# Rotary products from PSUM ahead of the root normalisation, in a fused attention and feed-forward kernel on Trainium2

## What is computed

```
xn = layernorm(x)
q  = (xn @ Wq.T) as 16 sub-heads of 8 numbers;  k likewise
rmsnorm(q) = q * rsqrt(mean(q*q over 8) + eps)
rotary: (x1, x2) -> (x1*c + x2*s, -x1*s + x2*c)       c, s by token
q, k = rotary(rmsnorm(q)), rotary(rmsnorm(k))
scores = q k^T, causal softmax, difference of two heads, times v, layernorm, Wproj
```

## Time and profile before

| | |
|---|---|
| median of 3 runs | 759.69 us |
| the profiled execution: span, first to last instruction | 687.9 us |
| mean granted TensorE clock | 0.950 |
| busy, PE / DVE / ACT / POOL | 590.2 / 530.8 / 496.5 / 326.7 us |
| projection stage | 0 to 116.6 us |
| attention with first feed-forward | 116.6 to 455.6 us |
| second block | 455.6 to 687.9 us |

### The profile page before, as it was taken

How to read it: one execution, slowest core, us unless ns; L and a number is a source line. 1 busy time by engine, 2 the same in 40 slices (tenths; PEclk the granted TensorE clock), 3 DMA queues, 4 the chain that set the end, 5 groups by cost and what they waited for, 6 DMA issues and landing times. The chain is left out here.

```text
span 687.9 us, 15892 instructions
## 1 busy us (share of the span) xinstructions
PE 590.2 (86%) x4825; PEld 355.3 (52%) x4826; DVE 530.8 (77%) x1425; ACT 496.5 (72%) x843; POOL 326.7 (47%) x466
## 2 busy tenths in 40 slices
PE   3576765899999999999999999977999799999960
PEld 2465554233333333333333333375877589999960
DVE  3999998687978889797888877779798856555575
ACT  2367795798989989898998999923455467777741
POOL 0224345344534344452434544252477777776661
PEclk9799998799999999999999999998899979999995
DMA  8000001000544566644466650041122233333475
GB/s 218 16 16 31 20 13 61 1 1 2 102 91 74 82 116 116 115 88 91 63 106 116 116 106 12 1 157 59 59 82 74 80 82 102 95 103 91 131 208 166
DMA packets 76265, 56.06 MB, mean 81 GB/s; under 512 B 6528, under 2 KB 70848, under 8 KB 75968
## 3 DMA queue, kind: packets, MB, share of 16 engines
q1 hardware_dynamic: 70688, 46.01, 30.8%
q0 software_dynamic: 4352, 8.99, 3.9%
q10 hardware_dynamic: 1184, 0.56, 0.3%
HBM read 15.36 MB, written 28.65 MB: 64 GB/s over the span
## 5 line engine op out<-in xcount | busy, mean ns | idle before, releaser
L787 ACT ACTIVATE attend_prob<-attend_ring 128x1024 f32<-128x1024 f32 (+1 forms) x320 | 280.0, 951 | 16.4 <-PE attend_ring L933 14.4
L731 POOL TENSOR_SCALAR_AFFINE_SELECT attend_prob<-attend_prob 128x256 f32<-128x256 f32 x256 | 118.0, 485 | 141.4 <-ACT attend_prob L787 140.8
L953 PE MATMUL attend_ps_o<-attend_prob,attend_v_slot 128*32 128x512 f32 (+3 forms) x1536 | 156.6, 496 | 0.0
L933 PE MATMUL attend_ring<-attend_qk_slot 32*128 32x512 f16 (+3 forms) x672 | 80.1, 329 | 8.1 <-ACT attend_prob L787 6.3
L1907 POOL DMA_INDIRECT expert_outputs<-routed_linear_gated,routed_expert_goal_now x72 | 70.3, 977 | 29.7 <-issue 23.9
L1033 POOL DMA_INDIRECT slots<-rows,slot_index x64 | 62.1, 971 | 37.3 <-issue 33.2
L933 PEld LDWEIGHTS attend_ring<-attend_qk_slot 32*128 32x128 f16 x672 | 22.4, 91 | 106.7 <-ACT attend_prob L787 37.6
L1935 DVE TENSOR_TENSOR outed_linear_head_normed<-outed_linear_head_normed,routed_linear_ps_c 128x256 f32<-128x256 f32 x72 | 30.2, 420 | 41.3 <-ACT outed_linear_head_normed L2029 36.8
L953 PEld LDWEIGHTS attend_ps_o<-attend_prob,attend_v_slot 128*32 128x32 f32 x1536 | 33.7, 108 | 44.9 <-issue 37.7
L2076 PE MATMUL routed_linear_ps_c<-outed_linear_head_normed,head_turned 128*128 128x128 f32 x384 | 52.5, 281 | 1.1 <-ACT head_turned L2010 1.1
L369 POOL TENSOR_TENSOR project_parts_q<-project_rotated_q,project_parts_q 128x1024 f16<-128x1024 f32 x8 | 17.6, 2201 | 68.9 <-ACT project_parts_q L417 68.9
(11 more groups left out here) (291 smaller groups left out, 1281.8 us busy)
## 6 DMA issues: line engine op xcount, KB each, us to landing
slots<-attend_zeros SPq DMA_DIRECT2D x24, 715.0 KB, 10.2
attend_qk_slot<-qk_parts SPq DMA_DIRECT2D x14, 512.0 KB, 3.1
x_pairs<-slots SPq DMA_DIRECT2D x72, 65.0 KB
v_all<-expert_outputs SPq DMA_DIRECT2D x8, 512.0 KB, 5.5
xn_all<-project_xn SPq DMA_DIRECT2D x8, 256.0 KB, 2.3
w<-w_laid SPq DMA_DIRECT2D x1, 2048.0 KB, 7.8
rows<-rows SPq DMA_DIRECT2D x4, 512.0 KB, 3.8
out<-xn_all SPq DMA_DIRECT2D x8, 256.0 KB, 3.5
```

The costliest lines, as they stand in the source:

```text
L731: ins = nc.gpsimd.affine_select(out=edge, in_=edge, compare_op=ALU.is_ge, fill=0.0, base=0, pattern=[[0, 2], [1, P]], channel_multiplier=-1)
L787: nc.scalar.activation(probs(k, pair)[:, :, 0:width], scores[:, :, 0:width], ACT.Exp, scale=HD ** -0.5).then_inc(exp_made[u][pair], 1)
L933: ins = nc.tensor.matmul(dst[:, s * QC + at:s * QC + at + cols], qk[rows, T + j * P:T + (j + 1) * P], qk[rows, qc * QC + off:(qc + 1) * QC ...
L953: ins = nc.tensor.matmul(ps_o[RB * s:RB * (s + 1), off:QC], v4[slot][:, j, s], probs(k, s // 2)[:, s % 2, at:at + cols], start=j == 0, sto ...
```

## The change

The rotary products are taken from the PSUM banks before the normalisation, in two halves (`turn_half`), each as soon as ScalarE has squared and copied that half; they move from group c, a turn later, to group b, behind the statistics of a and ahead of its normalisation. The additions (`add_halves`) follow the sum of squares of b, and the reciprocal of the root comes last in the turn. The product with the reciprocal root moves to GpSimd (`unit`), one operation of 512 columns for q and one for k, ahead of the low parts of the same group. ScalarE takes squares and v copies ahead of the deviation, both high parts follow each other and wait for GpSimd's products, and the root moves behind the copy of transposed x. TensorE's projections wait for `half_turned` in place of `half_normed`. A Sqrt of one column runs at the start.

```diff
@@ -212,69 +210,78 @@
         @block.vector
         def _(dve):
             def body(a, b, c, d):
-                if c:
-
-                    g, odd = c
-                    if isinstance(g, int) and g == 0:
-                        dve.wait_ge(rope_in, 16)
-                    dve.wait_ge(half_normed[1], g + 1)
-                    nc.vector.tensor_tensor(halves(qcos), halves(qkn), rope(odd, 0), ALU.mult)
-                    nc.vector.tensor_tensor(halves(qsin), halves(qkn), rope(odd, HD // 2), ALU.mult).then_inc(turned, 1)
...
-                if c:
-                    g, odd = c
-                    dve.wait_ge(turned, g + 1)
-                    once(dve, k_low, g)
-                    cs = qcos.rearrange("p (t w h s d) -> p t w h s d", t=GT, w=2, s=2, d=HD // 2)
-                    sn = qsin.rearrange("p (t w h s d) -> p t w h s d", t=GT, w=2, s=2, d=HD // 2)
-                    for w in range(2):
-                        r = rot[w].rearrange("p (t h s d) -> p t h s d", t=GT, s=2, d=HD // 2)
-                        nc.vector.tensor_tensor(r[:, :, :, 0], cs[:, :, w, :, 0], sn[:, :, w, :, 1], ALU.add)
-                        nc.vector.tensor_tensor(r[:, :, :, 1], cs[:, :, w, :, 1], sn[:, :, w, :, 0],
-                                                ALU.subtract).then_inc(rotated[w], 1)
+                    statistics(a)
+                if b:
+                    for h in range(2):
+                        turn_half(b, h)
...
                 if a:
...
+                    normalise(a)
                 if b:
-
                     g, odd = b
                     dve.wait_ge(squared, 2 * g + 2)
                     nc.vector.tensor_reduce(ssum, sq.rearrange("p (n d) -> p n d", d=HD), AX.X, ALU.add).then_inc(summed, 1)
-                if b:
-                    g, odd = b
+                    add_halves(b)
                     dve.wait_ge(rooted, g + 1)
+                    once(dve, unit_made[1], g)
                     nc.vector.reciprocal(rrms, sroot).then_inc(rrms_made, 1)
-                    dve.wait_ge(rrms_made, g + 1)
-                    for h in range(2):
-                        dve.wait_ge(v_kept[h], g + 1)
-                        tiles = slice(h * GT // 2, (h + 1) * GT // 2)
-                        ins = nc.vector.tensor_tensor(qkn.rearrange("p (t h d) -> p t h d", t=GT, d=HD)[:, tiles], qk_psum[:, tiles],
-                                                      bcast(rrms.rearrange("p (t h) -> p t h", t=GT)[:, tiles], 3, HD), ALU.mult)
-                        ins.then_inc(half_normed[h], 1)
...
+            def normalise(group):
+
+                g, odd = group
+                dve.wait_ge(sdev_made, g + 1)
+                nc.vector.reciprocal(rstd, sdev).then_inc(rstd_made, 1)
+                dve.wait_ge(rstd_made, g + 1)
+                once(dve, xn_saved[odd], (g - odd) * 8)
+                once(dve, x_turned, g - 1)
+                for j in range(GT):
+                    ins = nc.vector.tensor_scalar(xn[odd][:, j * P:(j + 1) * P], m.x[:, ds(g * GN + j * P, P)],
+                                                  moments[:, 2 * j:2 * j + 1], rstd[:, j:j + 1], ALU.subtract, ALU.mult)
+                ins.then_inc(normed, 1)
+
+            def turn_half(group, h):
+
+                g, odd = group
+                tiles = slice(h * GT // 2, (h + 1) * GT // 2)
+                if h == 0 and isinstance(g, int) and g == 0:
+                    dve.wait_ge(rope_in, 16)
+                numbers = qk_psum[:, tiles].rearrange("p t n (s d) -> p t (n s) d", s=2)
+                once(dve, rotated[1], g)
+                dve.wait_ge(v_kept[h], g + 1)
+                nc.vector.tensor_tensor(by_head(qcos)[:, tiles], numbers, rope(odd, 0)[:, tiles], ALU.mult)
+                nc.vector.tensor_tensor(by_head(qsin)[:, tiles], numbers, rope(odd, HD // 2)[:, tiles],
+                                        ALU.mult).then_inc(half_turned[h], 1)
+
+            def add_halves(group):
+
+                g, odd = group
+                dve.wait_ge(half_turned[1], g + 1)
+                cs = qcos.rearrange("p (t w h s d) -> p t w h s d", t=GT, w=2, s=2, d=HD // 2)
+                sn = qsin.rearrange("p (t w h s d) -> p t w h s d", t=GT, w=2, s=2, d=HD // 2)
+                for w in range(2):
+                    once(dve, unit_made[w], g)
+                    r = rot[w].rearrange("p (t h s d) -> p t h s d", t=GT, s=2, d=HD // 2)
+                    nc.vector.tensor_tensor(r[:, :, :, 0], cs[:, :, w, :, 0], sn[:, :, w, :, 1], ALU.add)
+                    nc.vector.tensor_tensor(r[:, :, :, 1], cs[:, :, w, :, 1], sn[:, :, w, :, 0],
+                                            ALU.subtract).then_inc(rotated[w], 1)
...
@@ -365,11 +372,19 @@
             def body(a, b, c, d):
                 if c:
                     g, odd = c
+                    pool.wait_ge(rrms_made, g + 1)
+                    lengths = rrms.rearrange("p (t w h) -> p t w h", t=GT, w=2)
+                    for w in range(2):
+                        once(pool, (q_low, k_low)[w], g)
+                        pool.wait_ge(rotated[w], g + 1)
+                        by_length = lambda x: x.rearrange("p (t h d) -> p t h d", t=GT, d=HD)
+                        nc.gpsimd.tensor_tensor(by_length(unit[w]), by_length(rot[w]), bcast(lengths[:, :, w], 3, HD),
+                                                ALU.mult).then_inc(unit_made[w], 1)
                     pool.wait_ge(q_high, g + 1)
-                    nc.gpsimd.tensor_tensor(part[odd][0][:, :, 2:4], bcast(rot_h[0], 2, 2), part[odd][0][:, :, 0:2],
+                    nc.gpsimd.tensor_tensor(part[odd][0][:, :, 2:4], bcast(unit_h[0], 2, 2), part[odd][0][:, :, 0:2],
                                             ALU.subtract).then_inc(q_low, 1)
                     pool.wait_ge(k_high, g + 1)
-                    nc.gpsimd.tensor_tensor(part[odd][1][:, :, 1::2], bcast(rot_h[1], 2, 2), part[odd][1][:, :, 0::2],
+                    nc.gpsimd.tensor_tensor(part[odd][1][:, :, 1::2], bcast(unit_h[1], 2, 2), part[odd][1][:, :, 0::2],
...
+            def square(group, h):
+
+                g, odd = group
+                act.wait_ge(qkv_made[h], g + 1)
...
             def body(a, b, c, d):
+                if b:
+                    square(b, 0)
+                    square(b, 1)
                 if a:
                     g, odd = a
                     act.wait_ge(mom_made, g + 1)
                     nc.scalar.activation(sdev, moments.rearrange("p (t k) -> p t k", k=2)[:, :, 1], ACT.Sqrt,
                                          bias=m.eps_ln[:, 0:1]).then_inc(sdev_made, 1)
-                if b:
-                    g, odd = b
...
                 if c:
                     g, odd = c
-                    act.wait_ge(rotated[0], g + 1)
-                    nc.scalar.activation(part[odd][0][:, :, 0:2], bcast(rot_h[0], 2, 2), ACT.Copy).then_inc(q_high, 1)
-                if b:
-                    g, odd = b
-                    act.wait_ge(summed, g + 1)
-                    nc.scalar.activation(sroot, ssum, ACT.Sqrt, bias=m.eps_rms[:, 0:1], scale=1.0 / HD).then_inc(rooted, 1)
-                if c:
-                    g, odd = c
-                    act.wait_ge(rotated[1], g + 1)
-                    nc.scalar.activation(part[odd][1][:, :, 0::2], bcast(rot_h[1], 2, 2), ACT.Copy).then_inc(k_high, 1)
+                    act.wait_ge(unit_made[0], g + 1)
+                    nc.scalar.activation(part[odd][0][:, :, 0:2], bcast(unit_h[0], 2, 2), ACT.Copy).then_inc(q_high, 1)
+                    act.wait_ge(unit_made[1], g + 1)
+                    nc.scalar.activation(part[odd][1][:, :, 0::2], bcast(unit_h[1], 2, 2), ACT.Copy).then_inc(k_high, 1)
...
                     nc.scalar.activation(xn_t[odd], ps_xt, ACT.Copy).then_inc(xt_kept, 1)
+                if b:
+                    g, odd = b
+                    act.wait_ge(summed, g + 1)
+                    nc.scalar.activation(sroot, ssum, ACT.Sqrt, bias=m.eps_rms[:, 0:1], scale=1.0 / HD).then_inc(rooted, 1)
...
             act.wait_ge(eps_made, 1)
+            nc.scalar.activation(warm, m.eps_ln, ACT.Sqrt)
             run(act, body, after)
...
@@ -482,7 +500,7 @@
                         pe.wait_ge(v_centred, 1)
                     pe.wait_ge(xt_kept, g + 1)
                     for h in range(2):
-                        once(pe, half_normed[h], g)
+                        once(pe, half_turned[h], g)
                         once(pe, v_kept[h], g)
                         for j in range(h * GT // 2, (h + 1) * GT // 2):
```

More of the change, by code:

```diff
@@ L127, in project_phase @@
         ssum, sroot, rrms = sb("qk_sum", GT * HQK), sb("qk_root", GT * HQK), sb("qk_rrms", GT * HQK)
-        qkn = sb("qk_normed", GT * HQK * HD)
         qcos, qsin = sb("qk_cos", GT * HQK * HD), sb("qk_sin", GT * HQK * HD)
-        rot = [sb(f"rotated_{n}", GT * SUB * HD) for n in "qk"]
+        rot, unit = ([sb(f"{what}_{n}", GT * SUB * HD) for n in "qk"] for what in ("rotated", "unit"))
```

(28 more changed lines are left out.)

37 lines of the change are left out of this document (11 added, 26 removed).

## The result

The changed kernel takes 783.46 us (median of 4 runs, 780.35 to 785.88) against 759.33 (4 runs, 758.86 to 761.22) beside it: a ratio of 1.035, interval 1.03 to 1.04. 780 us was forecast, with 762 to 788 as the range.

A forecast was written before the change was run, and what follows sets the result against it. VectorE was busiest, 10.07 of a 10.85 us steady turn in the projection phase. Waits for GpSimd (+11) and TensorE's lower clock (+9) took the span from 687.9 to 708 and 759.7 to 780 us; range 762 to 788.

The forecast's parts named there:

- L259 is of the form that waits: Projection phase: VectorE's four normalising operations, one SBUF input each, are held up by GpSimd's low parts of q and k.
- the fast form: Tensor_scalar form on VectorE that waits for GpSimd; L259 taken for it, 0.22 us at 128 columns plus 0.06 per operand.
- Rival (c): Normalisation in the projection phase: L259 doesn't wait for GpSimd at all; turn 9.25 or 9.65 us, time 755 us; chance 0.20.
- Two waits, not one: Normalisation: first L259 waits for q's low part (until 3.35), second for k's (5.4); the last two end at 6.05 instead of 2.65.
- V + 6.05: End of a turn's four L259, counted in us from the end of ScalarE's second V copy (V = 0).
- Rival (b): Normalisation: the four L259 pass as one with a single wait of 1.8 us; +0 to +7, 764 us; chance 0.13.
- A turn at full clock: Steady turn of the projection phase (one group of four token tiles): 12.64 us, 1.8 more than 10.85.
- The clock: TensorE idles 5.6 us each turn, so its clock drops: 1.4 us a spell, six to seven spells, +9, bounds 0 and +17.
- Rival (a): TensorE's clock holds in the projection phase, only the waits count: +11, 771 us; chance 0.13.
- The other terms of the waits: Projection phase: first reciprocal +2.4, six turns with the collision +10.8, seventh +1.9, tail -3.8; together +11.3 us.
- GpSimd's load: GpSimd in a steady turn: two unit products of 1.03 us each raise it from 4.25 to 6.3 us; no bound by its sum.
- 71.8 us around the span: Whole kernel: 71.8 us taken to lie around the profiled span of 687.9 us in the median of 759.69.

The follow-up runs named there:

- the first experiment: Changed kernel with GpSimd's low parts begun only behind the next group's additions: 754.63 us, ratio 1.0041 to the kernel before; again 757.14 us, 0.9978.
- the last experiment: Kernel of the first experiment, with VectorE making the last group's unit products and low parts itself: 750.98 us, ratio 0.9908 to the kernel before.

## Why the prediction was right

- **L259 is of the form that waits.** From an operand's price of 0.06 us the prediction took it for the fast form. Right: 2.153 us at most against 0.342, and the wait goes when GpSimd's operation is moved or cut. Rival (c) stood or fell with this.
- **Two waits, not one.** Done at V + 6.05 was forecast. The second V copy of this turn ended at 72.11 and L256 at 78.11, V + 6.00. The issue was at V + 1.72 instead of 1.52: I had left out the 0.20 us between the reciprocal and L259 that stand in the earlier trace rows. As the waits end with GpSimd's operations, this changed nothing. Rival (b), all four behind one wait, gives 2.9 us for L256 (issued at V + 1.52, normalised at 4.4). With one operation of GpSimd cut away it took 2.50, with both in place 4.28.
- **A turn at full clock** was put at 12.64 us; with the gap filled it is 12.51.
- **The clock.** 1.4 us for each spell: 13.94 less 12.51 is 1.4. In all +9 was forecast, and 9.0 measured by the same two kernels. The price of a spell was worked out; that the sum came out to the tenth is luck, since the bounds on record were 0 and +17. Rival (a) fell.
- **The other terms of the waits**, by the reciprocals of the roots (one each group) in the kernel with filler, against the profile of before. The first comes at 21.62 us instead of 18.72: +2.9, forecast +2.4, in which the early Sqrt stood with its whole 1.3 (alone it gave 0.3 to 0.7). From the first to the seventh 80.29 us instead of 67.41: +12.9, forecast 10.8. To the eighth 10.39 instead of 8.48: +1.9, as forecast. From the end of the eighth to the phase's end 16.7 instead of 21.1: -4.4, forecast -3.8. Together +13.3 against +11.3. The step that was short is the six turns: I walked one steady turn and took it six times, but the second took 15.3 us. There TensorE has 24 filler matmuls where the walked turn has 12, and behind a gap of 7.57 us they take 4.87 us at the low clock (0.50 from 30 to 35 us, 0.57 from 35 to 40) instead of 1.50. That this is all of the difference wasn't tested. With the clock the phase lost 22.3 us against 20.3 forecast, and the 2.0 us are these terms.
- **GpSimd's load.** 6.3 us a turn and 1.03 us for a unit product: 6.30, and 1.07. VectorE's products from PSUM take 0.60 us a step; in the first experiment, where all four of a turn are issued while GpSimd is at work (58.39 to 60.88 us), they do so too and don't wait, as the prediction read from L275.
- **Where it was wrong.** 71.8 us around the span was a misreading, and it did no harm, since the forecast was a difference added to the median. Had I scaled a share of the span, it would have. The measured difference of the medians is 24.1 us, that of the phase 22.3; the second block's own scatter (292 to 304 us) is larger than the rest.

The two rules of the Trainium skill that the prediction set beside the rows: on the shared port pair (SBUF — State Buffer, Who interferes with whom), that one of the two engines blocks for the other's whole instruction, L256 now shows it, 2.153 us against 0.342. The drain behind a table load (ScalarE: Activation LUTs, What ACT_TABLE_LOAD costs), 2.66 us in all, the rows don't show: the next ACTIVATE stands 1.30 us after the load's start.

## What to carry to other kernels

Work given to GpSimd is paid by when it runs, not by how much it is: the same 56 us of it cost 22 us of the kernel's time in one place and nothing in another. Before moving an operation there, list what VectorE issues while it runs, and see which of these forms the trace has ever shown beside a GpSimd operation; where the critical one is a short operation repeated, count one wait for each GpSimd operation that is ready, not one for the group. Then read the idle gap that this makes in TensorE against the gaps behind which the same trace shows its clock at 0.50.

## What the runs showed of the hardware that I had not expected

A GpSimd operation that only writes holds up L256 as well. In the kernel with short low parts GpSimd clears the buffers at the start:

```profile
5.92 1.80 POOL L404 MEMSET project_parts_q<- 128x2048 f16 x1
...
7.67 1.80 POOL L404 MEMSET project_parts_k<- 128x2048 f16 x1
```

```profile
7.37 2.75 DVE L256 TENSOR_SCALAR project_xn<-x,project_moments,project_rstd 128x128 f32<-128x128 f32 x4
```

The four L256 take 2.75 us instead of 1.1 and end 0.65 us after the second memset, which reads nothing. Nor does a small size protect: in the tail of the first experiment's kernel a tensor_scalar of 16 columns waits for the rest of a low part, and lasts 2.09 us (0.17 in the kernel before and in the last experiment's, where GpSimd rests then):

```profile
104.00 3.20 POOL L389 TENSOR_TENSOR project_parts_k<-project_unit_k,project_parts_k 128x1024 f16<-128x1024 f32 x1
105.14 2.09 DVE L308 TENSOR_SCALAR project_norm_exp<-project_norm_exp 128x16 f32<-128x16 f32 x1
```
